# Weighing two groups of key blocks in a row in a two-layer perceiver kernel, with exponentials six double blocks ahead

## The chip, the cores and the metric

The kernel runs on one core of one Trainium2 chip. The metric is the device time of one execution in microseconds (us), as the median of the runs. Engines are called PE (TensorE, matrix products), DVE (VectorE), ACT (ScalarE) and POOL (GpSimd); SP issues DMAs. Each works through its own list in order and meets the others only at semaphores.

## The reference, cut to what matters

Six stages, each added to a residual x of 2 batches of 256 tokens by 256 channels. Stages 0 and 3 are cross attentions over a context of 4096 keys, and the change is inside these two. All is float32.

```
# stage 0, 8 heads of 64 ("plain"); stage 3, 16 heads of 64 ("biased")
q, k, v = xn @ Wq, context @ Wk, context @ Wv
sim     = einsum('bihd,bjhd->bhij', q, k) * scale (+ bias[256, 4096] in stage 3)
out     = softmax(sim) @ v
x       = x + out @ Wo (+ bo in stage 0)
```

Stage 1 is a chunked delta rule, stage 2 a mixture of 15 experts, stage 4 an attention with quantised numbers, stage 5 a recurrent cell over 64 steps.

## The kernel before, in words

`cross_attention` (L161) serves both attention stages. A step m is one pair of heads of one batch: 8 steps in the plain stage and 16 in the biased one. The 4096 keys are 8 groups g of 512; a group is two double blocks kp of 256 keys each, 16 in all. Scores stand with keys on the partitions, so E has 16 slots of 128 x 1024 numbers, one for each double block.

The steps overlap. In the sweep of m (L412 on PE), PE weighs the values with the exponentials of m, computes the scores of m+1, and projects context pieces: the values of m+1 and the keys of m+2. In the text Wg is the weighing of group g (8 products, recorded as 16 instructions), Sg the scores of group g, and Vg and Kg are the projections (pieces) of its values and keys. The order is written out by hand: in each group come W, then in groups 2, 3 and 5 a V piece, then S, then one more piece, by the tables

```
BEFORE_SCORES = {2: ("V", 2), 3: ("V", 3), 5: ("V", 5)}
AFTER_SCORES = {0: ("V", 0), 1: ("V", 1), 2: ("K", 0), 3: ("K", 1), 4: ("V", 4), 5: ("K", 2), 6: ("K", 3), 7: ("K", 4)}
```

After group 7 follows the end of the sweep: V6, the sum over keys (L388), V7, the turning of the peaks (L394), K5, the spreading of the peaks (L399), the output projection (L407), K6, the queries of m+2, and K7.

Three rules decide who waits for whom.

- All pieces go through one PSUM bank (PIECE = 4). A piece waits until ACT has copied the one before it (`piece_kept`, L334).
- Scores alternate between two double banks: Scores of kp wait until those of kp-2 have been copied to E (`scores_kept`, L359). In the biased stage DVE copies them and adds the bias (L559, "out" in the text); in the plain stage ACT copies them (L505).
- After a step's scores, the peak of each query is found by DVE (L573), and each slot of E is lowered by it (DVE, L580), then goes through the exponential (ACT, L510), then is weighed (PE) and summed (POOL, L297). AHEAD = 4 slots are lowered at the end of the sweep. The others are lowered inside the next sweep: at its double block kp DVE lowers slot kp + 4, behind the out of kp; ACT's two exponentials of slots 2g + 4 and 2g + 5 stand in its list behind the copies of the pieces of group g.

The first sweep of a stage only scores, the last only weighs. The last but one has no more keys to compute, so only V pieces. So 6 sweeps of the plain stage and 14 of the biased one are complete.

Of the kernel before, what the change touches and what calls it, by code (L numbers as in the profile page):

```python
# [160 lines left out]
def cross_attention(nc, c, k, tag, wqkv, w_out, b_out, ctx_t, biased, heads, scale):  # L161
# [10 lines left out]
    KG = S2 // NG  # L172
    NP = 2 * NG
    HQ = 4
    AHEAD = 4
    V_PIECES = [piece for piece in PIECES if piece[0] == "V"]
    with ExitStack() as stack:
        def sb(name, shape, dtype=F32):
# [43 lines left out]
        def pieces_of(m):  # L222

            return V_PIECES if isinstance(m, int) and m == END - 2 else PIECES

        def piece_count(m, piece):

            return NP * m + 24 + pieces_of(m).index(piece) + 1
# [7 lines left out]
        def values_count(p, g):  # L236

            return piece_count(p - 1, ("V", g))
# [15 lines left out]
        with nc.Block() as block:  # L254
# [54 lines left out]
            def _(pe):  # L309
# [20 lines left out]
                def piece(m, which):  # L330
                    if which not in pieces_of(m):
                        return
                    kind, g = which
                    pe.wait_ge(piece_kept, piece_count(m, which) - 1)  # L334
                    if kind == "V":
                        values(m + 1, g)
                    else:
                        keys(m + 2, g, PIECE)
# [30 lines left out]
                def weigh(m, g):  # L369
                    pe.wait_ge(piece_kept, values_count(m, g))  # L370
                    if g == 0 and not (isinstance(m, int) and m == START):
                        pe.wait_ge(o_kept, m)
                    for kp in (2 * g, 2 * g + 1):
                        pe.wait_ge(exp_done, NP * m + kp + 1)
                        for h in range(2):
                            for n in range(2):
                                last = pe.matmul(c.ps[n * HD:(n + 1) * HD, OUT, h * S:(h + 1) * S],  # L377
                                                 VS[:, 2 * kp + n, h * HD:(h + 1) * HD], E[:, kp, 2 * h:2 * h + 2, n, :],
                                                 start=(kp == 0 and h == 0), stop=(kp == NP - 1),
                                                 skip_group_check=True)  # L380
                    if g == NG - 1:
                        last.then_inc(weighed, 1)

                def spread_sums(m, scoring):
                    pe.wait_ge(summed, NP * m + NP)
                    if scoring:
                        pe.wait_ge(scores_kept, NP * (m + 1) + NP - 1)
                    pe.matmul(c.ps[:, SUMS_SPREAD, :], c.ones[:, :], FOLD[:, :, :].rearrange("p a n -> p (a n)"),  # L388
                              start=True, stop=True).then_inc(sums_spread, 1)
# [21 lines left out]

                def sweep(m, attending, scoring, more_keys):  # L412
                    for g in range(NG):
                        if attending:
                            weigh(m, g)
                        if scoring:
                            if g in BEFORE_SCORES:
                                piece(m, BEFORE_SCORES[g])
                            scores(m + 1, 2 * g)
                            scores(m + 1, 2 * g + 1)  # L420
                            piece(m, AFTER_SCORES[g])
                    if scoring:
                        piece(m, ("V", 6))
                    if attending:
                        spread_sums(m, scoring)
                    if scoring:
                        piece(m, ("V", 7))
                        turn_peaks(m + 1)
                        piece(m, ("K", 5))
                        spread_peaks(m + 1)  # L430
                    if attending:
                        project(m)
                    if more_keys:
                        piece(m, ("K", 6))
                        queries(m + 2)
                        piece(m, ("K", 7))
# [42 lines left out]
            @block.scalar  # L479
            def _(act):  # L480
                def keys_out(count, g, bank):
                    act.wait_ge(piece_done, count)
                    act.activation(KT[:, g * KG:(g + 1) * KG], c.ps[:, bank, :], ACT.Copy).then_inc(piece_kept, 1)  # L483

                def piece_out(m, which):
                    if which not in pieces_of(m):
                        return
                    kind, g = which
                    count = piece_count(m, which)
                    if kind == "K":  # L490
                        keys_out(count, g, PIECE)
                    else:
                        act.wait_ge(piece_done, count)
                        act.activation(VS[:, 4 * g:4 * g + 4, :].rearrange("p a n -> p (a n)"), c.ps[:, PIECE, :],  # L494
                                       ACT.Copy).then_inc(piece_kept, 1)

                def queries_out(p):
                    act.wait_ge(q_done, p + 1)
                    act.activation(QS[:, :], c.ps[:, QUERIES, 0:S], ACT.Copy, scale=scale).then_inc(q_kept, 1)

                def scores_out(p, kp, attending):
                    act.wait_ge(scores_done, NP * p + kp + 1)
                    if attending:
                        act.wait_ge(summed, NP * (p - 1) + max(kp, 1))
                    act.activation(both(E[:, kp, :, :, :]), scores_bank(kp), ACT.Copy).then_inc(scores_kept, 1)  # L505

                def exponential(p, kp):
                    act.wait_ge(lowered, NP * p + kp + 1)
                    at = both(E[:, kp, :, :, :])
                    act.activation(at, at, ACT.Exp).then_inc(exp_done, 1)  # L510

                def sweep(m, attending, scoring, more_keys):
                    for g in range(NG):
                        if scoring:
                            if g in BEFORE_SCORES:
                                piece_out(m, BEFORE_SCORES[g])
                            if not biased:
                                scores_out(m + 1, 2 * g, attending)
                                scores_out(m + 1, 2 * g + 1, attending)
                            piece_out(m, AFTER_SCORES[g])  # L520
                        if attending and 2 * g + AHEAD < NP:
                            exponential(m, 2 * g + AHEAD)
                            exponential(m, 2 * g + AHEAD + 1)
                    if scoring:
                        piece_out(m, ("V", 6))
                        piece_out(m, ("V", 7))
                        piece_out(m, ("K", 5))
                        exponential(m + 1, 0)
                        piece_out(m, ("K", 6))
                        exponential(m + 1, 1)  # L530
                        if more_keys:
                            queries_out(m + 2)
                        piece_out(m, ("K", 7))
                        exponential(m + 1, 2)
                        exponential(m + 1, 3)

                if b_out is not None:
                    act.dma_start(bo[:, :], b_out.rearrange("(o n) -> o n", o=1)).then_inc(rest_in, 16)
                norm_scalar(c, act, k)

                act.wait_ge(c.ln_std, k + 1)
                keys_out(NP * START + 1, 0, PIECE)
                keys_out(NP * START + 2, 1, PIECE + 1)
                queries_out(START)
                for g in range(2, NG):
                    keys_out(NP * START + g + 1, g, PIECE + g % 4)
                sweep(START - 1, False, True, True)
                with act.Fori(START, END - 2) as m:
                    sweep(m, True, True, True)
                sweep(END - 2, True, True, False)  # L550
                sweep(END - 1, True, False, False)

            @block.vector
            def _(dve):
# [53 lines left out]
                def sweep(m, attending, scoring):  # L608
                    for kp in range(NP):
                        if scoring and kp > 0:  # L610
                            peak(m + 1, kp - 1, 0)
                        if scoring and biased:
                            scores_out(m + 1, kp, attending)
                            if kp > 0:
                                peak(m + 1, kp - 1, 1)
                        if attending and kp + AHEAD < NP:
                            lower(m, kp + AHEAD)
                        if scoring and not biased and kp > 0:
# [11 lines left out]
                    if scoring:  # L630
                        for kp in range(AHEAD):
                            lower(m + 1, kp)
# [1437 lines left out]
```

## Time and profile before

| | |
|---|---|
| median of 3 runs | 2179.23 us (2177.58 to 2181.44) |
| profiled execution | 2181.46 us, of which the span is 2179.7 us |
| PE busy | 1920.6 us (88%) |
| DVE busy | 1632.9 us (75%) |
| POOL busy | 956.5 us (44%) |
| ACT busy | 838.5 us (38%) |
| mean granted TensorE clock | 0.934 of full speed |

A matmul's record is longer than the step to the next one, since matmuls are pipelined. So the cost of a block on PE is read as the distance from its start to the start of the next block; "idle before" counts only the time after the modelled end. Times of the trace count from the start of the span. The plain attention takes about the first 590 us, the biased one runs from about 930 to 2015 us.

### The profile page before, as it was taken

The page shows a single profiled execution, that of the slowest core. Times are in us where ns is not written, and L with a number is a line of the kernel's source. Part 1 is how long each engine was busy: PE and PEld are TensorE (multiplying, and loading weights), DVE is VectorE, ACT ScalarE, POOL GpSimd, SP SyncE. Part 2 cuts the span into 40 slices and gives each one's busy share as a digit, 9 for nine tenths or more (in the row PEclk, how much of TensorE's full clock was granted, in tenths as well). Part 3 has the DMA queues.
Part 4 walks back from the last instruction along what each step waited for, and adds up shares of the span by engine and source line. Part 5 has one row for each costly group of instructions (what it writes and reads, how often), then busy time and mean ns, then how long its engine had stood idle before and what let it go on. Part 6 is the DMA issues. An engine that isn't in the chain of part 4 may idle for free. (4 is left out here: it accounts for less than half of the span.)

```text
span 2179.7 us, 34477 instructions
## 1 busy us (share of the span) xinstructions
PE 1920.6 (88%) x12512; PEld 1311.0 (60%) x12514; DVE 1632.9 (75%) x2131; ACT 838.5 (38%) x1108; POOL 956.5 (44%) x450
## 2 busy tenths in 40 slices
PE   8999999999458889899999999999999999996226
PEld 5666666666238778666666666666666666664124
DVE  3666666668387356689988999889998889987562
ACT  3655665556230135233343333433343333434001
POOL 0454665546550034024655546555465545646200
PEclk9999999999669589999999999999999999998557
DMA  2000100000100062000000000110000000000001
GB/s 104 8 13 12 58 31 12 12 8 6 40 3 1 1 242 77 10 8 8 5 12 12 12 5 7 54 47 12 0 12 12 12 12 0 12 8 5 20 0 49
DMA packets 27717, 52.45 MB, mean 24 GB/s; under 512 B 4227, under 2 KB 15252, under 8 KB 27156
## 3 DMA queue, kind: packets, MB, share of 16 engines
q1 hardware_dynamic: 27200, 51.60, 7.3%
q8 instruction: 34, 0.56, 0.1%
q10 hardware_dynamic: 468, 0.16, 0.0%
q14 instruction: 15, 0.12, 0.0%
HBM read 51.23 MB, written 0.52 MB: 24 GB/s over the span
## 5 line engine op out<-in xcount | busy, mean ns | idle before, releaser
L297 POOL TENSOR_TENSOR biased_sums<-biased_sums,biased_scores 128x1024 f32<-128x1024 f32 x224 | 529.2, 2363 | 210.0 <-ACT biased_scores L510 205.9
L559 DVE TENSOR_TENSOR biased_scores<-ps,bias 128x1024 f32<-128x1024 f32 x256 | 311.0, 1215 | 79.4 <-PE ps L365 79.4
L510 ACT ACTIVATE biased_scores<-biased_scores 128x1024 f32<-128x1024 f32 x256 | 268.2, 1053 | 245.0 <-DVE biased_scores L580 244.0
L573 DVE TENSOR_TENSOR ps<-ps,biased_scores 128x512 f32<-128x512 f32 x480 | 331.6, 691 | 3.6
L580 DVE TENSOR_TENSOR biased_scores<-biased_scores,ps 128x1024 f32<-128x1024 f32 x256 | 304.9, 1210 | 11.9 <-PE ps L399 11.9
L297 POOL TENSOR_TENSOR plain_sums<-plain_sums,plain_scores 128x1024 f32<-128x1024 f32 x112 | 264.6, 2362 | 84.5 <-ACT plain_scores L510 74.7
L325 PEld LDWEIGHTS ps<-weights_again,context_again 128*128 128x128 f32 x2048 | 238.2, 191 | 70.2 <-issue 33.5
L325 PE MATMUL ps<-weights_again,context_again 128*128 128x128 f32 x2048 | 262.4, 281 | 13.1 <-ACT biased_keys L483 11.0
L316 PE MATMUL ps<-context_again,weights_again 128*128 128x512 f32 x512 | 251.3, 613 | 19.5 <-ACT biased_values L494 16.9
L365 PE MATMUL ps<-biased_queries,biased_keys 64*128 64x256 f32 x2048 | 257.3, 390 | 6.6 <-DVE biased_scores L559 5.8
L573 DVE TENSOR_TENSOR ps<-ps,plain_scores 128x512 f32<-128x512 f32 x240 | 167.3, 697 | 115.7 <-ACT plain_scores L505 111.4
L377 PE MATMUL ps<-biased_scores,biased_values 128*64 128x256 f32 x2048 | 250.8, 386 | 1.8 <-ACT biased_scores L510 1.1
L365 PEld LDWEIGHTS ps<-biased_queries,biased_keys 64*128 64x128 f32 x2048 | 186.7, 186 | 63.1 <-DVE biased_scores L559 24.4
L377 PEld LDWEIGHTS ps<-biased_scores,biased_values 128*64 128x64 f32 x2048 | 135.4, 136 | 123.4 <-issue 59.6
L297 POOL TENSOR_TENSOR biased_sums<-biased_scores 128x1024 f32<-128x1024 f32 x16 | 37.8, 2364 | 356.9 <-ACT biased_scores L510 356.9
L483 ACT ACTIVATE biased_keys<-ps 128x512 f32<-128x512 f32 x128 | 76.5, 597 | 280.1 <-PE ps L316 280.1
L316 PEld LDWEIGHTS ps<-context_again,weights_again 128*128 128x128 f32 x512 | 88.0, 189 | 116.7 <-issue 88.3
L580 DVE TENSOR_TENSOR plain_scores<-plain_scores,ps 128x1024 f32<-128x1024 f32 x128 | 152.1, 1211 | 7.0 <-PE ps L399 7.0
L494 ACT ACTIVATE biased_values<-ps 128x512 f32<-128x512 f32 x128 | 75.7, 591 | 178.5 <-PE ps L325 178.5
L505 ACT ACTIVATE plain_scores<-ps 128x1024 f32<-128x1024 f32 x128 | 124.0, 1020 | 43.2 <-PE ps L365 43.2
L325 PEld LDWEIGHTS ps<-weights,context 128*128 128x128 f32 x1024 | 119.1, 191 | 35.7 <-issue 16.4
L325 PE MATMUL ps<-weights,context 128*128 128x128 f32 x1024 | 131.2, 281 | 7.6 <-ACT plain_keys L483 5.5
(356 smaller groups left out, 2304.1 us busy)
## 6 DMA issues: line engine op xcount, KB each, us to landing
context<-in_ctx_t SPq DMA_DIRECT2D x8, 1024.0 KB, 5.4
moe_w<-in_moe_w SPq DMA_DIRECT2D x32, 256.0 KB, 2.8
context_again<-in_ctx_t SPq DMA_DIRECT2D x8, 1024.0 KB, 6.6
weights_again<-in_wqkv SPq DMA_DIRECT2D x45, 128.0 KB, 2.1
bias<-in_fside SPq DMA_DIRECT2D x1, 4096.0 KB, 22.6
biased_w_out<-in_w_out SPq DMA_DIRECT2D x16, 256.0 KB, 2.6
weights<-in_wqkv SPq DMA_DIRECT2D x21, 128.0 KB, 2.1
plain_w_out<-in_w_out SPq DMA_DIRECT2D x8, 256.0 KB, 2.7
```

Of the source, the lines that this page charges most:

```text
L297: pool.tensor_tensor(both(SUM[:, :, :, :]), both((E[:, 0] if kp == 1 else SUM)[:, :, :, :]), both(E[:, kp, :, :, :]), ALU.add).then_inc(su ...
L316: last = pe.matmul(c.ps[:, bank, :], W[:, 1, i, :], CT[:, i, g * KG:(g + 1) * KG], start=(i == 0), stop=(i == DC - 1))
L325: last = pe.matmul(c.ps[:, PIECE, n * P:(n + 1) * P], CT[:, i, g * KG + n * P:g * KG + (n + 1) * P], W[:, 2, i, :], start=(i == 0), stop=( ...
L365: last = pe.matmul(out, KT[half, at:at + P], QS[half, :].rearrange("p (t j) -> p t j", t=2), start=True, stop=True)
L377: last = pe.matmul(c.ps[n * HD:(n + 1) * HD, OUT, h * S:(h + 1) * S], VS[:, 2 * kp + n, h * HD:(h + 1) * HD], E[:, kp, 2 * h:2 * h + 2, n, :],
L483: act.activation(KT[:, g * KG:(g + 1) * KG], c.ps[:, bank, :], ACT.Copy).then_inc(piece_kept, 1)
L494: act.activation(VS[:, 4 * g:4 * g + 4, :].rearrange("p a n -> p (a n)"), c.ps[:, PIECE, :], ACT.Copy).then_inc(piece_kept, 1)
L505: act.activation(both(E[:, kp, :, :, :]), scores_bank(kp), ACT.Copy).then_inc(scores_kept, 1)
L510: act.activation(at, at, ACT.Exp).then_inc(exp_done, 1)
L559: dve.tensor_tensor(E[:, kp, :, :, :].rearrange("p (h t) n j -> p h t (n j)", h=2), scores_bank(kp).rearrange("p (h t n) -> p h t n", h=2, ...
L573: ins = dve.tensor_tensor(to, highest, E[:, kp, :, n, :], ALU.max)
L580: dve.tensor_tensor(at, at, c.ps[:, LOWER, :].rearrange("p (a j) -> p a j", a=HQ).unsqueeze(2) .to_broadcast([P, HQ, 2, P]), ALU.add).then ...
```

## The change

Before even groups PE weighs that group and the next one; before odd groups it weighs none. AHEAD becomes 6: six slots are lowered, and six exponentials are done, at the end of a sweep, and in group g of the next one stand the exponentials of slots 2g + 6 and 2g + 7.

```diff
-    AHEAD = 4
+    AHEAD = 6
@@ PE
                 def sweep(m, attending, scoring, more_keys):
                     for g in range(NG):
-                        if attending:
+                        if attending and g % 2 == 0:
                             weigh(m, g)
+                            weigh(m, g + 1)
                         if scoring:
                             if g in BEFORE_SCORES:
                                 piece(m, BEFORE_SCORES[g])
@@ ACT
                         piece_out(m, ("K", 7))
-                        exponential(m + 1, 2)
-                        exponential(m + 1, 3)
+                        for kp in range(2, AHEAD):
+                            exponential(m + 1, kp)
```

On PE, in the loop of the biased stage, group 3 before: weighing (L377), V3 (L325), scores (L365), K1 (L316).

```order
L316 MATMUL ps<-context_again,weights_again 128x512 x2
L370 REGISTER_ALU
L374 REGISTER_ALU
L377 MATMUL ps<-biased_scores,biased_values 64x256 x4
L374 REGISTER_ALU
L377 MATMUL ps<-biased_scores,biased_values 64x256 x4
L334 REGISTER_ALU
L325 MATMUL ps<-weights_again,context_again 128x128 x8
L350 REGISTER_ALU
L359 REGISTER_ALU
L365 MATMUL ps<-biased_queries,biased_keys 128x2x128 x4
```

The same place now:

```order
L316 MATMUL ps<-context_again,weights_again 128x512 x2
L334 REGISTER_ALU
L325 MATMUL ps<-weights_again,context_again 128x128 x8
L350 REGISTER_ALU
L359 REGISTER_ALU
L365 MATMUL ps<-biased_queries,biased_keys 128x2x128 x4
```

The weighing between the piece K0 (L316, first row) and the piece V3 (L325) has moved to group 2, and the two pieces stand side by side. The same holds for V4 and V5 in groups 4 and 5.

On ACT, in the same loop, from the copy of V5 (L494) on, before: the copies of V5 and K2, two exponentials (L510, slots 14 and 15), the copies of K3 and K4.

```order
L494 ACTIVATE biased_values<-ps 128x512
L482 REGISTER_ALU
L483 ACTIVATE biased_keys<-ps 128x512
L508 REGISTER_ALU
L510 ACTIVATE biased_scores<-biased_scores 128x1024
L508 REGISTER_ALU
L510 ACTIVATE biased_scores<-biased_scores 128x1024
L482 REGISTER_ALU
L483 ACTIVATE biased_keys<-ps 128x512
```

From the copy of V4 (L495) on, now:

```order
L495 ACTIVATE biased_values<-ps 128x512
L509 REGISTER_ALU
L511 ACTIVATE biased_scores<-biased_scores 128x1024
L509 REGISTER_ALU
L511 ACTIVATE biased_scores<-biased_scores 128x1024
L494 REGISTER_ALU
L495 ACTIVATE biased_values<-ps 128x512
L483 REGISTER_ALU
L484 ACTIVATE biased_keys<-ps 128x512
```

The exponentials ahead of the copy of V5 are now those of slots 14 and 15, where they were those of 12 and 13; behind the copy of K2 there are none.

## Rows read from the trace of the kernel before

**Rows 1.** Windows: length, busy us of PE, PEld, DVE, ACT, POOL; PEclk.
```profile
214.52:281.98 67.46, 66.35 (x437) 43.74 (x436) 45.22 (x54) 40.57 (x49) 36.70 (x17) 1.00 0.22 71
1035.09:1103.63 68.54, 66.48 (x438) 43.76 (x437) 62.07 (x69) 25.62 (x33) 36.72 (x17) 1.00 0.03 10
```
**Rows 2.** Waits of PE: total us, times, longest; biased (two rows), then plain stage.
```profile
PE ps L316 <- ACT biased_values L494: 16.7, 42, 0.7
PE ps L325 <- ACT biased_keys L483: 9.6, 14, 0.7
...
PE ps L325 <- ACT plain_keys L483: 4.1, 6, 0.7
```
**Rows 3.** Timeline of PE, biased sweep: start, us, instructions, idle before.
```profile
1035.09 1.95 PE L377 MATMUL ps<-biased_scores,biased_values 128*64 128x256 f32 x16
1036.96 2.00 PE L365 MATMUL ps<-biased_queries,biased_keys 64*128 64x256 f32 x16
1038.89 2.05 PE L325 MATMUL ps<-weights_again,context_again 128*128 128x128 f32 x16
1040.87 1.95 PE L377 MATMUL ps<-biased_scores,biased_values 128*64 128x256 f32 x16
...
1052.72 1.98 PE L316 MATMUL ps<-context_again,weights_again 128*128 128x512 f32 x4 [0.21 <-ACT biased_values L494]
1054.63 1.95 PE L377 MATMUL ps<-biased_scores,biased_values 128*64 128x256 f32 x16
...
1074.71 1.98 PE L316 MATMUL ps<-context_again,weights_again 128*128 128x512 f32 x4 [0.74 <-ACT biased_values L494]
...
1088.82 2.05 PE L325 MATMUL ps<-weights_again,context_again 128*128 128x128 f32 x16 [0.69 <-ACT biased_keys L483]
...
1091.57 2.04 PE L325 MATMUL ps<-weights_again,context_again 128*128 128x128 f32 x16
...
1096.46 1.12 PE L399 MATMUL ps<-biased_peaks_diagonal,ones 128*128 128x512 f32 x2 [0.18 <-DVE biased_peaks_diagonal L594]
```
**Rows 4.** Timeline of PE: the end of W0 in two short windows, and K6.
```profile
1036.21 0.82 PE L377 MATMUL ps<-biased_scores,biased_values 128*64 128x256 f32 x6
...
1036.43 0.60 PE L377 MATMUL ps<-biased_scores,biased_values 128*64 128x256 f32 x4
...
1099.15 1.88 PE L316 MATMUL ps<-context_again,weights_again 128*128 128x512 f32 x4
1100.86 1.03 PE L343 MATMUL ps<-XNT,weights_again 128*128 x4
```
**Rows 5.** Timeline of ACT, same sweep.
```profile
1035.68 1.99 ACT L510 ACTIVATE biased_scores<-biased_scores 128x1024 f32<-128x1024 f32 x2
1040.98 0.60 ACT L494 ACTIVATE biased_values<-ps 128x512 f32<-128x512 f32 x1 [3.30 <-PE ps L325]
...
1073.11 1.06 ACT L510 ACTIVATE biased_scores<-biased_scores 128x1024 f32<-128x1024 f32 x1 [2.40 <-DVE biased_scores L580]
1074.08 0.58 ACT L494 ACTIVATE biased_values<-ps 128x512 f32<-128x512 f32 x1
```
**Rows 6.** Timeline of DVE, same sweep.
```profile
1029.08 4.62 DVE L580 TENSOR_TENSOR biased_scores<-biased_scores,ps 128x1024 f32<-128x1024 f32 x4 [0.62 <-PE ps L399]
...
1038.24 1.22 DVE L559 TENSOR_TENSOR biased_scores<-ps,bias 128x1024 f32<-128x1024 f32 x1 [3.95 <-PE ps L365]
...
1041.11 1.22 DVE L559 TENSOR_TENSOR biased_scores<-ps,bias 128x1024 f32<-128x1024 f32 x1
...
1044.56 1.22 DVE L559 TENSOR_TENSOR biased_scores<-ps,bias 128x1024 f32<-128x1024 f32 x1
...
1082.98 1.21 DVE L559 TENSOR_TENSOR biased_scores<-ps,bias 128x1024 f32<-128x1024 f32 x1
...
1085.49 1.23 DVE L559 TENSOR_TENSOR biased_scores<-ps,bias 128x1024 f32<-128x1024 f32 x1
...
1091.77 3.36 DVE L585 RECIPROCAL biased_shares<-ps 128x512 f32<-128x512 f32 x1 [0.53 <-PE ps L388]
```

## The prediction

> **What bounds the kernel now.** I read the page's busy shares first: PE 88%, DVE 75%. They are means over stages, so next come windows over one complete sweep of each attention [rows 1]. The reader sees that PE is busy for 66.35 of 67.46 us (plain) and 66.48 of 68.54 us (biased), at full granted clock, with DVE at 45 us in the one and 62 us in the other. So PE sets the pace. In the biased stage DVE has only 6.5 us to spare, and it feeds ACT, which feeds PE. Third, what PE waits for: ACT's copies of pieces. The 42 waits of the first row are three in each of 14 biased sweeps, and the 14 of the second are one in each [rows 2]. The timeline shows these places: 0.21 us before K0, 0.74 before K2, 0.69 before V6 [rows 3]. The 0.69 is the pure price of two pieces in a row through one bank: K4 runs, ACT copies for 0.6 us, V6 starts. The 0.74 is another thing. The copy of V5 came at 1074.08, behind the exponential at 1073.11, which had waited for DVE's lowering [rows 5]. So a copy can be late because of its place in ACT's list.
>
> **Prices.** PE, start to next start [rows 3]: W 1.88 and 1.87, S 1.93, V before W 1.98, K before W 1.91. A piece right behind a piece starts 1.98 + 0.69 = 2.67 us after a K, and 2.75 after a V (V6 to V7 is 1091.57 - 1088.82, with a product between them that does not use the bank; by the copy alone, 2.09 + 0.60 + 0.05 = 2.74). ACT starts a V copy 2.09 us after V starts [rows 3, 5] and takes 0.6; a pair of exponentials takes 1.99, one 1.06, and the next instruction follows after 0.97 [rows 5]. DVE: the out of kp starts 1.28 us after its S for an even kp (1038.24 - 1036.96), out 0 to out 1 is 2.87, later ones 3.45 with a lowering between and 2.51 without; a lowering takes 1.2, with steps of 1.13 [rows 6].
>
> **W next to W.** No such pair ran before at full clock. Inside W, each two records are 0.22 us apart (1036.21 to 1036.43), but the last two start at 1036.65 and S only at 1036.96: 0.31 [rows 3, 4]. So 0.10 of W's 1.88 is the passage to another block, and 8 x 0.216 = 1.73 is its own, which leaves 0.05 at its entry. K6, followed by a block of its own tile form, lasts 1.71 (1099.15 to 1100.86), against 1.91 before W [rows 3, 4]. Bounds for two Ws: 3.76 (nothing saved) and 3.44 (both at K6's pace). I take 3.61, from W's own rows: 0.15 saved, four times a sweep, so 0.6 us per sweep. The Trainium skill ("TensorEngine Tiling (Array Packing)", Key Properties) says that changing the tiling mode drains the engine, and the trace agrees with these 0.10 to 0.20 us. By that rule alone the change would only gain.
>
> **The biased sweep now**, from the start of W0 = 0. At the end of the sweep before, six lowerings start at -6.0 (1029.08) and end at 0.9, and ACT does exponentials 2 to 5 from 0.6 to 4.5. W1 needs 2 at 1.8 and 3 at 2.6; they end at 1.65 and 2.6. No stall, but no margin.
> - S0 3.6, V0 5.5, S1 7.5. DVE starts out 0 at 4.9 and out 1 at 7.8, done at 9.0. S1's second half is ready at 8.5 and waits: stall 0.55. Before, W1 stood between S0 and S1 and hid this.
> - V1 10.0, W2 12.0, W3 13.8, V2 15.6, S2 17.6, K0 19.5. The copy of V2 stands behind exponential 9 (lowering 9 ends at 17.6), and is done at 19.2, so the old 0.21 before K0 is gone.
> - V3 directly behind K0: 22.2 instead of 21.4, stall 0.76. S3 24.15.
> - K1 is ready at 26.1. The copy of V3 now stands behind exponential 11. Out 4 could start only at 18.85, since S2 was late; out 5 follows at 22.3, lowering 11 ends at 25.25, exponential 11 at 26.3, the copy at 26.8. K1 starts at 26.9: stall 0.80.
> - W4 28.8, W5 30.6, S4 32.4, V4 34.3, V5 37.1: stall 0.75. S5 39.0. The copy of V5 stands behind exponential 15: out 8 starts at 33.7, out 9 at 37.1, lowering 15 ends at 40.1, the copy at 41.65. K2 is ready at 41.0, starts at 41.7: stall 0.74, as before.
> - W6 43.6, W7 45.4, S6 47.2, K3 49.2, S7 51.1 with 0.2 for out 13, K4 53.2, V6 55.9 (the old 0.75 between them stays).
> - Before, V6 started 53.73 after W0 [rows 1, 3]. Then V6 to L399 was 7.64. DVE has been fed late: out 15 starts at 56.0, its peaks end at 59.2, L399 comes 4.69 behind the reciprocal [rows 3, 6], at 63.9, so 8.0 behind V6. From there to the next W0 7.17 as before.
> The sweep is 71.06 us instead of 68.54: 2.5 more. As a sum: new stalls 0.55 + 0.76 + 0.80 + 0.75 + 0.2 = 3.06, less 0.21 removed and 0.6 saved by W next to W, plus 0.3 at the end. 14 complete sweeps: 35 us.
>
> **The plain sweep now.** ACT copies the scores there, and DVE only has lowerings and peaks, so slots are lowered well ahead: the copies of V3 and V5 (24 and 38 us after W0) find exponentials 11 and 15 done. What is new is V3 behind K0, 0.76, and V5 behind V4, 0.75; the plain V6 behind K4 has the same 0.7 today [rows 2]. Less 0.6: 0.9 a sweep, 5.6 us in 6.
>
> **The other sweeps.** The first ones do not weigh, the last ones only weigh: the order is as before, and the two lowerings more at the end of a sweep are two fewer later. The sweep with V pieces only: in the plain stage 0.75 for V4 and V5 and some 0.3 for two score blocks in a row, less 0.6; in the biased stage DVE sets the pace, as 14 us of its 19 us of lowerings lie in the sweep, now 11, and the later start of S0 takes that back. Together 0.8. POOL sums at 2.4 us a slot, 36.7 of 68.5 us [rows 1]; it ends well before the sweep does. SP's loads wait for the same pieces.
>
> **Sum.** 35 + 5.6 + 0.8 = 41.4 us on the profiled 2181.46 gives 2222.9; on the median of the runs, which is 2.2 lower, 2220.6. I predict 2221 us.
>
> **Rivals.**
> - Only the shared bank counts. The biased copies of V3 and V5 come early enough, and DVE isn't starved: biased 0.76 + 0.75 - 0.21 - 0.6 = 0.7 a sweep, plus plain 5.6: 15 us, 2195. For it: DVE stood idle for 3.95 us before out 0 [rows 6] and now lowers two slots there. Against: S2 and S4 come late on PE, so DVE can't start outs 4 and 8 earlier. Chance 0.12.
> - DVE's chain snowballs: the exponentials of the head slots come late for W1, S1's stall grows to the full 1.3 us from S to out, and the late DVE carries its delay past L399. Then 1.2 us more in each biased sweep, 17 us: 2238. If two Ws also save nothing, 2250. For it: the margins at W1 are 0 to 0.1. Chance 0.12.
> - No change: V3 and V5 cost their 1.5 a sweep, but an earlier V5 copy also removes the 0.74 before K2, and two Ws save 0.32, the lower bound, four times: biased 1.5 - 0.95 - 1.3 = -0.7, plain 0.2, together 9 us less at most, or about zero with the stall of S1. About 2179. Chance 0.05.
> - Faster: the drain is what counts. If ACT's copy between neighbouring pieces lay beside PE's drain, the two new stalls would be under 0.3 each and the rest would be 0.6 + 0.95 gained per biased and 0.6 per plain sweep, less 0.6: 14 x 0.95 = 13 us less, 2166. It decides from the point where a pair of pieces costs less than W next to W saves. Against: the 0.69 before V6 stands in all 14 sweeps [rows 2]. Chance 0.04. The skill's rule on the tiling mode, above, is the one that speaks for it.
> - The granted clock falls since PE idles more. It was 1.00 with 2.1 us idle in a sweep [rows 1]; now it's 4.5 in pieces under 1 us. I give this nothing of its own; it is in the upper end.
>
> **How the numbers follow.** Forecast 0.67, the rivals 0.12, 0.12, 0.05, 0.04. The forecast's own bounds come from two Ws (3.44 to 3.76, so 14 us less to 12 us more over 20 sweeps) and from 0.3 us a sweep on each stall that ends by DVE. The range takes in both near rivals in part: 2193 to 2238. A measurement of this kernel tells 0.2%, about 4 us, from no change. Faster 0.05, same 0.05, slower 0.90.
>
> **What would show it.** Right: 71.1 us between two L399 in the biased stage, 68.4 in the plain; idle of PE near 0.7 before V3, K1, V5, K2 and V6, and 0.5 in S1 behind DVE; none before K0; two Ws in 3.6. Wrong: no idle before K1, or L399 to L399 under 70 us; PE idle over 1 us at W1 or S1; a granted clock under 1.00 in complete sweeps.

## The result and the profile after

The changed kernel takes 2219.1 us (median; 2218.1 to 2220.4) against 2179.2 before: ratio 1.0183, 95% interval 1.0165 to 1.020, so a loss that is clear of the noise. That is 39.9 us more, where 2221 was forecast. The profiled execution took 2220.4 us, with a span of 2218.6.

Windows over one plain and one biased sweep after, with the columns of [rows 1]:

```profile
216.00:284.44 68.44, 65.95 (x438) 43.97 (x436) 45.44 (x54) 40.35 (x49) 36.75 (x17) 1.00 0.22 70
1116.54:1187.61 71.07, 66.64 (x438) 43.81 (x436) 62.24 (x70) 25.41 (x34) 36.79 (x17) 1.00 0.03 9
```

The lengths are 68.44 and 71.07 us, against 67.46 and 68.54. Busy times hardly differ: PE does the same work in a longer sweep. The granted clock is 1.00 in both.

The waits of PE in the biased stage after (total us, times, longest), to be read against [rows 2]:

```profile
PE ps L316 <- ACT biased_values L495: 23.2, 43, 0.7
PE ps L325 <- ACT biased_keys L484: 19.2, 28, 0.7
PE ps L325 <- ACT biased_values L495: 10.3, 15, 0.7
PE ps L365 <- DVE biased_scores L560: 10.3, 19, 1.4
PE ps L399 <- DVE biased_peaks_diagonal L595: 8.6, 15, 3.9
```

The keys row went from 14 waits to 28: V3 behind K0 is the new one. The third row is new: V5 behind V4. The fourth now has one wait of 0.37 us in each complete sweep, S1's; its other five lie in the sweep with V pieces only. The timeline of PE from W0 to L399 of one biased sweep (start, us, instructions, idle before) shows each step:

```profile
1115.67 3.73 PE L377 MATMUL ps<-biased_scores,biased_values 128*64 128x256 f32 x32
1119.33 2.00 PE L365 MATMUL ps<-biased_queries,biased_keys 64*128 64x256 f32 x16
...
1123.24 1.14 PE L365 MATMUL ps<-biased_queries,biased_keys 64*128 64x256 f32 x8
1124.74 1.14 PE L365 MATMUL ps<-biased_queries,biased_keys 64*128 64x256 f32 x8 [0.37 <-DVE biased_scores L560]
1125.81 2.05 PE L325 MATMUL ps<-weights_again,context_again 128*128 128x128 f32 x16
1127.79 3.67 PE L377 MATMUL ps<-biased_scores,biased_values 128*64 128x256 f32 x32
1131.39 2.05 PE L325 MATMUL ps<-weights_again,context_again 128*128 128x128 f32 x16
...
1135.30 1.98 PE L316 MATMUL ps<-context_again,weights_again 128*128 128x512 f32 x4
1137.97 2.05 PE L325 MATMUL ps<-weights_again,context_again 128*128 128x128 f32 x16 [0.69 <-ACT biased_keys L484]
...
1142.68 1.98 PE L316 MATMUL ps<-context_again,weights_again 128*128 128x512 f32 x4 [0.73 <-ACT biased_values L495]
...
1152.86 2.05 PE L325 MATMUL ps<-weights_again,context_again 128*128 128x128 f32 x16 [0.69 <-ACT biased_values L495]
...
1157.50 1.98 PE L316 MATMUL ps<-context_again,weights_again 128*128 128x512 f32 x4 [0.66 <-ACT biased_values L495]
...
1166.86 2.30 PE L365 MATMUL ps<-biased_queries,biased_keys 64*128 64x256 f32 x16
1169.09 1.98 PE L316 MATMUL ps<-context_again,weights_again 128*128 128x512 f32 x4
1171.76 2.05 PE L325 MATMUL ps<-weights_again,context_again 128*128 128x128 f32 x16 [0.69 <-ACT biased_keys L484]
...
1179.56 1.13 PE L399 MATMUL ps<-biased_peaks_diagonal,ones 128*128 128x512 f32 x2 [0.33 <-DVE biased_peaks_diagonal L595]
```

To be read in it, in this order: two Ws in 3.66 (the first pair) or 3.60 to 3.61 us (the others), where two took 3.75 or 3.76; S1's second half waiting for DVE, so that S1 takes 2.57 us (1123.24 to 1125.81) where an S takes 1.93; no idle before K0 at 1135.30, where 0.21 stood; the new 0.69 before V3, 0.73 before K1 and 0.69 before V5; 0.66 before K2 and 0.69 before V6, which were there before (0.74 and 0.69) [rows 3]; S7 in 2.23 us instead of 1.93 (1166.86 to 1169.09); and L399 0.33 late, where it was 0.18. V6 comes 56.1 us after W0.

The wait before K1 is in ACT's list. Its timeline there:

```profile
1137.82 1.05 ACT L511 ACTIVATE biased_scores<-biased_scores 128x1024 f32<-128x1024 f32 x1
1141.09 1.06 ACT L511 ACTIVATE biased_scores<-biased_scores 128x1024 f32<-128x1024 f32 x1 [2.22 <-DVE biased_scores L581]
1142.05 0.58 ACT L495 ACTIVATE biased_values<-ps 128x512 f32<-128x512 f32 x1
```

V3 was computed by 1140.02 (1137.97 + 2.05), but exponential 11 waited 2.22 us for DVE's lowering, and V3's copy stood behind it until 1142.05.

### The profile page after: what moved, and what is told of

Same layout as the page of the kernel before. It is cut to its first block and busy times, and to the rows that moved or that the text cites. A ratio compares the mean times of both kernels' runs of the same rounds, so it can differ in the third digit from the quotient of the medians.

```text
span 2218.6 us, 34465 instructions
## 1 busy us (share of the span) xinstructions
PE 1916.5 (86%) x12512; PEld 1311.8 (59%) x12514; DVE 1636.8 (74%) x2131; ACT 833.6 (38%) x1108; POOL 957.5 (43%) x450
## 5 line engine op out<-in xcount | busy, mean ns | idle before, releaser
L325 PEld LDWEIGHTS ps<-weights_again,context_again 128*128 128x128 f32 x2048 | 238.2, 192 | 93.4 <-ACT biased_keys L484 45.4
L325 PE MATMUL ps<-weights_again,context_again 128*128 128x128 f32 x2048 | 262.5, 281 | 33.0 <-ACT biased_keys L484 20.6
L365 PE MATMUL ps<-biased_queries,biased_keys 64*128 64x256 f32 x2048 | 265.8, 393 | 12.7 <-DVE biased_scores L560 11.2
L316 PE MATMUL ps<-context_again,weights_again 128*128 128x512 f32 x512 | 251.4, 614 | 25.8 <-ACT biased_values L495 23.2
L377 PE MATMUL ps<-biased_scores,biased_values 128*64 128x256 f32 x2048 | 238.2, 384 | 1.5 <-ACT biased_scores L511 0.7
L365 PEld LDWEIGHTS ps<-biased_queries,biased_keys 64*128 64x128 f32 x2048 | 184.3, 186 | 81.3 <-issue 32.0
L377 PEld LDWEIGHTS ps<-biased_scores,biased_values 128*64 128x64 f32 x2048 | 138.7, 137 | 108.7 <-issue 38.4
L316 PEld LDWEIGHTS ps<-context_again,weights_again 128*128 128x128 f32 x512 | 88.1, 189 | 123.0 <-issue 79.8
L495 ACT ACTIVATE biased_values<-ps 128x512 f32<-128x512 f32 x128 | 75.6, 591 | 193.5 <-PE ps L325 193.5
L325 PEld LDWEIGHTS ps<-weights,context 128*128 128x128 f32 x1024 | 119.1, 192 | 45.9 <-ACT plain_keys L484 21.2
L325 PE MATMUL ps<-weights,context 128*128 128x128 f32 x1024 | 131.3, 281 | 16.5 <-ACT plain_keys L484 9.6
```

The costliest lines, as they stand in the source:

```text
L316: last = pe.matmul(c.ps[:, bank, :], W[:, 1, i, :], CT[:, i, g * KG:(g + 1) * KG], start=(i == 0), stop=(i == DC - 1))
L325: last = pe.matmul(c.ps[:, PIECE, n * P:(n + 1) * P], CT[:, i, g * KG + n * P:g * KG + (n + 1) * P], W[:, 2, i, :], start=(i == 0), stop=( ...
L365: last = pe.matmul(out, KT[half, at:at + P], QS[half, :].rearrange("p (t j) -> p t j", t=2), start=True, stop=True)
```

## Experiments

The length of a sweep is read below from the rows of L399 (its number moves by a few lines with the code), which runs once a sweep, recorded as two instructions 0.56 us apart: first and last start, less 0.56, over the number of sweeps between.

**AHEAD back at 4, weighing still in pairs.**

```diff
-    AHEAD = 6
+    AHEAD = 4
```

> The changed kernel with AHEAD back at 4: two groups weighed in a row, but only four slots exponentiated ahead. Theory A (AHEAD = 6 is what pays for the pairs: the second W of a pair needs exponentials that DVE lowers two double blocks later): W3 waits about 4 us for exponential 7, W5 and W7 about 1.8 us each, and a biased sweep is near 78 us instead of 71.07; the plain sweep, where DVE lowers well ahead, stays within 0.3 us of 68.44. Total about 2320 us. Theory B (the loss of the change comes from the six lowerings at the end of the sweep, which fill DVE there): the biased sweep comes back to under 70 us, total about 2200 us.

Measured 2396.9 us in a single run, before 2181.0 on the same chip. The plain sweep is 68.9 us, the biased one 81.9. The row of L399 (one biased sweep between four records) and the timeline of PE from W2 to K0, with the second half of W5:

```profile
L399 PE MATMUL ps<-biased_peaks_diagonal,ones x4: 592/645/697, 1299.8 to 1382.3; 128*128 128x512 f32 x4
```

```profile
1319.12 1.95 PE L377 MATMUL ps<-biased_scores,biased_values 128*64 128x256 f32 x16
1322.35 1.08 PE L377 MATMUL ps<-biased_scores,biased_values 128*64 128x256 f32 x8 [1.28 <-ACT biased_scores L511]
1325.81 1.98 PE L377 MATMUL ps<-biased_scores,biased_values 128*64 128x256 f32 x8 [2.37 <-ACT biased_scores L511]
1327.71 3.79 PE L325 MATMUL ps<-weights_again,context_again 128*128 128x128 f32 x16
1331.43 2.27 PE L365 MATMUL ps<-biased_queries,biased_keys 64*128 64x256 f32 x16
1333.63 1.98 PE L316 MATMUL ps<-context_again,weights_again 128*128 128x512 f32 x4
...
1347.44 1.08 PE L377 MATMUL ps<-biased_scores,biased_values 128*64 128x256 f32 x8 [1.71 <-ACT biased_scores L511]
```

Theory A: W3 waits for exponentials 6 and 7 (1.28 and 2.37 us), and W5 and W7 wait 1.71 us each. Six slots ahead are what makes pairs bearable in the biased stage. The plain sweep came out 0.47 us above 68.44, a little more than the 0.3 allowed. The size was missed, since something was added that nobody had written down: behind the 2.37 us of idle the same eight records take 1.98 us, not 1.08, and V2 3.79, not 2.05. The windows of this stretch have the granted clock (third column from the end):

```profile
1300.00:1320.00 20.00, 19.63 (x126) 13.09 (x128) 13.65 (x16) 8.69 (x12) 10.53 (x5) 1.00 0.11 33
1325.30:1325.80 0.50, 0.00 (x0) 0.00 (x0) 0.00 (x0) 0.45 (x1) 0.00 (x0) 0.50 0.00 0
1325.80:1330.00 4.20, 4.19 (x18) 3.06 (x19) 0.00 (x0) 0.00 (x0) 2.35 (x1) 0.50 0.00 0
1332.10:1332.50 0.40, 0.40 (x8) 0.35 (x6) 0.00 (x0) 0.03 (x1) 0.00 (x0) 1.00 0.00 0
```

It fell from 2.4 to 1.2 GHz while PE still waited, and was back by 1332.1, nearly 7 us later. Over that time PE lost 2.9 us: 0.9 in the eight records, 1.7 in V2 (1327.71 to 1331.43 is 3.72 for 1.98) and 0.3 in S2 (2.20 for 1.93). The rest of the 10.9 us above 71.07 is the waits: counted from start to start W2 and W3 lost 4.1 us, W4 with W5 and W6 with W7 1.9 each. So the waits were near what was expected, and the clock is what was left out.

**AHEAD = 6 alone, one group weighed at a time.**

```diff
# kernel before
-    AHEAD = 4
+    AHEAD = 6
-                        exponential(m + 1, 2)
-                        exponential(m + 1, 3)
+                        for kp in range(2, AHEAD):
+                            exponential(m + 1, kp)
```

> The kernel before with AHEAD = 6 alone, weighing one group at a time as before. Theory A (the lowering two slots earlier moves nothing that PE waits for: ACT's exponentials of a group still wait for DVE's work of the same double block): biased sweep 68.5 us, plain sweep 67.5 us, total 2179 us within 5; the 0.74 us before K2 stays. Theory B (six lowerings at the end are part of the loss): biased sweep 69 us or more, total over 2187 us.

Measured 2175.7 us against 2181.0, ratio 0.9978 (0.9967 to 0.9989). L399 over two sweeps, this kernel and the kernel before:

```profile
L399 PE MATMUL ps<-biased_peaks_diagonal,ones x6: 592/644/697, 1095.4 to 1233.0; 128*128 128x512 f32 x6
```

```profile
L399 PE MATMUL ps<-biased_peaks_diagonal,ones x6: 592/644/697, 1096.5 to 1234.1; 128*128 128x512 f32 x6
```

Both are (137.6 - 0.56) / 2 = 68.5 us, and the plain sweep is 67.47 in both. So AHEAD = 6 by itself moves no complete sweep: theory A. The last but one biased sweep, which has V pieces only and where DVE sets the pace, is 2.0 us shorter (64.8 against 66.8), which fits the two slots that DVE now lowers in its idle time before it starts. The two profiled spans differ by 6.8 us. Of these, 2.0 are this sweep, and 3.7 lie behind the last L399 of the biased stage (189.2 against 192.9 us), where nobody changed anything and where the eight executions of this document differ by as much among themselves (last section). So beyond the 2.0 us it is open how much of the gain comes from AHEAD = 6.

**Copies between the exponentials, weighing in pairs.** In the biased stage ACT copies V2, V3 and V5 between the two exponentials of the group before.

```diff
-                            if g in BEFORE_SCORES:
+                            if g in BEFORE_SCORES and not (biased and attending):
                                 piece_out(m, BEFORE_SCORES[g])
...
                             exponential(m, 2 * g + AHEAD)
+                            if scoring and biased and g + 1 in BEFORE_SCORES:
+                                piece_out(m, BEFORE_SCORES[g + 1])
                             exponential(m, 2 * g + AHEAD + 1)
```

> The changed kernel; in the biased stage ACT copies V2, V3 and V5 between the two exponentials of the group before, instead of behind both. Theory A (the waits before K1 and K2 are the copies' place in ACT's list, behind exponentials 11 and 15): both waits vanish (0.73 + 0.66 us), the 0.69 us before V3 and V5 stay, the biased sweep falls from 71.07 to about 69.5 us, 14 x 1.5 = 21 us less: about 2198 us. Theory B (DVE sets the pace of the biased sweep now, and PE's waits only show it): the time taken away before K1 and K2 comes back before S3, S5 or L399, and the sweep stays over 70.7 us, total over 2213 us.

Measured 2200.8 us, ratio 1.0094 (1.0079 to 1.011). L399 over two sweeps, then PE from S3 to K1 and from V5 to K2:

```profile
L399 PE MATMUL ps<-biased_peaks_diagonal,ones x6: 592/644/697, 1105.0 to 1244.6; 128*128 128x512 f32 x6
```

```profile
1136.47 2.00 PE L365 MATMUL ps<-biased_queries,biased_keys 64*128 64x256 f32 x16
1138.40 1.98 PE L316 MATMUL ps<-context_again,weights_again 128*128 128x512 f32 x4
...
1148.58 2.05 PE L325 MATMUL ps<-weights_again,context_again 128*128 128x128 f32 x16 [0.69 <-ACT biased_values L495]
1150.56 2.00 PE L365 MATMUL ps<-biased_queries,biased_keys 64*128 64x256 f32 x16
1152.49 1.98 PE L316 MATMUL ps<-context_again,weights_again 128*128 128x512 f32 x4
```

A sweep is 69.5 us. K1 follows S3 without idle, and K2 too (1150.56 to 1152.49), while the 0.69 before V3 and V5 stays. So 1.5 us a sweep are gained without touching PE's order. Not all of that is loss of the change: the wait before K2 was there before it. Theory B falls: DVE, at 62 us of 69.5, didn't ask for the time elsewhere, and the waits that it ends, 0.37 us in S1 and 0.33 before L399, are as they were.

**The same edit of ACT's list in the kernel before.** (AHEAD = 4, one group at a time.)

> The kernel before (single weighings, AHEAD = 4) with the same edit of ACT's list: V2, V3 and V5 copied between two exponentials in the biased stage. Theory A: the 0.21 us before K0 and the 0.74 us before K2 go, the biased sweep falls from 68.54 to 67.7 us, the end of the sweep gives back 0.1 to 0.2; 14 x 0.8 = 11 us less: about 2168 us. Theory B (DVE, busy for 62 of 68.5 us, is at its limit): the waits move to DVE's products (S or L399) and the sweep stays within 0.2 us of 68.54, total 2177 to 2181 us.

Measured 2164.8 us against 2181.0, ratio 0.9928 (0.9914 to 0.9941).

```profile
L399 PE MATMUL ps<-biased_peaks_diagonal,ones x6: 592/644/697, 1095.5 to 1231.2; 128*128 128x512 f32 x6
```

```profile
1139.30 2.00 PE L365 MATMUL ps<-biased_queries,biased_keys 64*128 64x256 f32 x16
1141.23 1.98 PE L316 MATMUL ps<-context_again,weights_again 128*128 128x512 f32 x4
```

A sweep is 67.6 us instead of 68.5. K2 now starts 1.93 us behind S5, where it was 2.73: the 0.74 us before K2 was the place of V5's copy behind an exponential. The 0.21 before K0 is gone too, and L399 waits 0.30 instead of 0.18.

With the copies between the exponentials in both kernels, pairs cost 69.5 - 67.6 = 1.9 us a sweep, against 2.5 with the copies behind. So the place of the copies accounts for 0.6 us of the loss that the change brings, and PE's order, by the shared bank and by DVE, for the other 1.9.

**Pairs with the pieces spread.** The changed kernel (AHEAD = 6, copies in their old place), with no two pieces side by side in groups 0 to 7 (the list of all pieces, put in the same order, is left out here):

```diff
+BEFORE_SCORES = {2: ("V", 2), 4: ("V", 4), 6: ("K", 2)}
+AFTER_SCORES = {0: ("V", 0), 1: ("V", 1), 2: ("V", 3), 3: ("K", 0), 4: ("V", 5), 5: ("K", 1), 6: ("K", 3), 7: ("K", 4)}
```

> The changed kernel (pairs, AHEAD = 6) with the same 11 pieces in the sweep put where no two are neighbours: W0 W1 S0 V0 S1 V1 W2 W3 V2 S2 V3 S3 K0 W4 W5 V4 S4 V5 S5 K1 W6 W7 K2 S6 K3 S7 K4. Theory A (the bank shared by neighbouring pieces is what the plain stage loses, and W next to W saves 0.6 us there): no wait before V3 and V5, plain sweep 66.9 us, so below the 67.46 of single weighing; biased sweep about 70.2, since scores two blocks apart make PE wait about 1 us for DVE before the second halves of S1, S3 and S5. Total about 2197 us. Theory B (W next to W saves nothing in a whole sweep, and the plain loss is of another cause): plain sweep 67.5 us or more.

Measured 2204.5 us, ratio 1.0111 (1.0094 to 1.0128). L399 over one plain and two biased sweeps, and the waits for DVE in the biased stage:

```profile
L399 PE MATMUL ps<-plain_peaks_diagonal,ones x4: 592/644/697, 138.9 to 206.4; 128*128 128x512 f32 x4
...
L399 PE MATMUL ps<-biased_peaks_diagonal,ones x6: 592/645/697, 1095.7 to 1237.2; 128*128 128x512 f32 x6
```

```profile
PE ps L365 <- DVE biased_scores L560: 33.5, 44, 1.0
PE ps L325 <- ACT biased_keys L484: 9.6, 14, 0.7
```

The plain sweep is 66.9 us, 1.5 below the changed kernel's 68.44 and 0.55 below the 67.46 of single weighing. This is both halves of the plain sum at once: two pairs of neighbouring pieces cost 1.5 us, and four pairs of Ws save 0.55. The biased sweep is only 0.6 us shorter, 70.5: PE now waits for DVE before the second halves of S1, S3 and S5 (0.37, 0.96, 0.96 us), because scores stand closer together than DVE's 6.9 us for a group. So in the biased stage pairs lost in both orders of pieces that were run; other orders were not. The total is 7.5 us above the expected 2197: 4 of them are the 0.3 us by which each biased sweep is longer than expected, and the rest was in the expectation, whose own sweeps add up to about 2200.

**What the runs point to.** The plain stage with pairs and spread pieces; the biased stage with single weighings and the copies between the exponentials; AHEAD = 6 in both.

> What the runs point to: plain stage with pairs and spread pieces, biased stage with single weighings and the copies of V2, V3 and V5 between two exponentials, AHEAD = 6 in both. Theory A (the parts are independent): plain sweep 66.9 us, biased sweep 67.6 us, the sweep with V pieces only 2 us shorter as with AHEAD = 6 alone; about 2160 us, 1% below the kernel before. Theory B (AHEAD = 6 takes from DVE at the end of the sweep what the new place of the copies gave): biased sweep 68 us or more, total over 2166 us.

Measured 2161.3 us (2157.1 to 2165.6) against 2180.1, ratio 0.9907 (0.9891 to 0.9924): faster than both kernels.

```profile
L406 PE MATMUL ps<-biased_peaks_diagonal,ones x6: 592/644/697, 1098.0 to 1233.4; 128*128 128x512 f32 x6
```

The biased sweep is 67.4 us, the plain one 66.92: theory A, the parts are independent. Against the copies' edit alone (0.9928) the two intervals overlap, so the total does not prove the last 3 us; the sweeps do. In its profiled execution, the slowest of the four, the stages between the two attentions took 431.5 us, against 425.1 in the kernel before, though no one touched them; the granted clock (third column from the end) was lower there:

```profile
532.90:964.40 431.50, 336.54 (x2283) 270.11 (x2282) 260.39 (x440) 112.67 (x198) 111.04 (x75) 0.80 0.15 48
```

```profile
535.60:960.70 425.10, 329.38 (x2282) 263.08 (x2281) 260.21 (x440) 112.61 (x198) 111.04 (x75) 0.83 0.14 49
```

## Why the prediction was right

The direction, the places and the size were right. The biased sweep as a sum, in us against the kernel before. Measured is from start to start of the blocks, the measure that the prediction names for costs; the idle column reads up to 0.3 us less, as it counts from a modelled end.

| term | forecast | measured |
|---|---|---|
| S1's second half waits for DVE | +0.55 | +0.64 |
| V3 behind K0 | +0.76 | +0.76 |
| K1, V3's copy behind exponential 11 | +0.80 | +0.80 |
| V5 behind V4 | +0.75 | +0.75 |
| S7 waits for out 13 | +0.2 | +0.30 |
| K0, its old wait gone | -0.21 | -0.27 |
| K2, V5's copy behind exponential 15 | 0 | -0.08 |
| W next to W, four pairs | -0.6 | -0.54 |
| end of the sweep | +0.3 | +0.16 |
| sum | +2.55 | +2.52 |

- **What bounds.** PE in both stages, with ACT's copies ending its waits: confirmed: the busy time of a sweep is unchanged and the waits grew.
- **Two Ws.** 3.61 forecast; 3.60 to 3.61 for three pairs and 3.66 for the first. The spread pieces show the saving in a whole sweep, 0.55 of 0.6 us.
- **S1.** The second half starts 1.50 us after the first, where without a wait it starts after 0.97 (1042.75 to 1043.72 before), so it comes 0.53 us late. The forecast of 0.55 met that. But the eight records behind the wait then take 1.07 us instead of 0.96, which makes 0.64; the prediction left those 0.1 us out, here and in S7.

```profile
1042.75 2.00 PE L365 MATMUL ps<-biased_queries,biased_keys 64*128 64x256 f32 x16
1043.72 1.03 PE L365 MATMUL ps<-biased_queries,biased_keys 64*128 64x256 f32 x8
```

- **Copies behind exponentials 11 and 15.** Both waits are there, and both are gone when only ACT's list is edited. The prediction set K2 down as unchanged at 0.74, a number of the idle column; from start to start it was 0.80 before and is 0.72.
- **The end of the sweep.** L399 came 7.8 behind V6, not 8.0, and V6 at 56.1, not 55.9. That the sum met 2.52 within 0.03 is partly luck: single terms missed by up to 0.14, and these misses cancel.
- **The plain sweep.** 0.9 forecast, 0.98 seen.
- **The sweeps with V pieces only.** 0.8 forecast for the two together, 1.5 seen. The plain one was put at 0.45 and lost 1.2; half of that is the wait for L399 at its end, which grew from 2.66 to 3.24 us and which the prediction did not count.
- **Sum.** The trace gives 14 x 2.53 + 6 x 0.98 = 41.3 us in the complete sweeps and 1.5 in the other two, so the attention stages lost about 43 us, a little more than forecast. The span grew by only 38.9 us, since behind the biased stage the profiled execution was 3.7 us shorter, as the last section tells. So the forecast 41.4 lies near the 39.9 of the medians partly by luck.

Of the rivals, "only the shared bank counts" was wrong in its own terms. It gave 0.7 us a biased sweep with the wait before K2 still there. The kernel with copies between the exponentials has 69.5 - 68.5 = 1.0 without that wait, where the rival would then give about 0. What it leaves out is DVE: S1, S7 and the end of the sweep, together 1.1 us. "DVE's chain snowballs" did not come, but the margin was used up: in the sweep above, exponential 3 ended at about 1118.27, W1's second half, which needs it, started at 1118.32, and the first pair took 0.06 us more than the others.

## What to carry to other kernels

When an order is changed, look for what the moved block stood between: here W's 1.9 us hid a 0.7 us hand-over of a shared PSUM bank between two pieces. Look also at where a copy that frees a bank stands in its engine's list: behind an instruction that waits for a third engine it comes late. Three such copies moved ahead gave 0.7%, more than any regrouping here; by PE's rows V5's copy gave 0.8 of the 0.95 us a sweep. And a walk through one period, row by row on three engines, forecast the length of a sweep within 0.1 us, and most of its terms too.

## What the runs showed of the hardware

- A block on TensorE behind a block of other tile form cost 0.1 to 0.2 us more than behind one of its own: two Ws in a row took 3.60 us instead of 3.76, and four such pairs saved 0.55 us in a plain sweep. No run separates the form of the tiles from other differences between the blocks. It agrees in kind with the rule that the prediction cites from the Trainium skill ("TensorEngine Tiling (Array Packing)", Key Properties), that a change of the tiling mode drains the engine; the size is from these rows.
- With AHEAD = 4 and pairs, TensorE waited 1.28 us, worked for 1.1 and waited 2.37; before the second wait was over the granted clock was 0.50, and stayed so for nearly 7 us. Waits of 1.71 us, once in each later pair, left it at 1.00, and so did the 0.7 us pauses of the changed kernel, five in a sweep.
- Stages that nobody touched differ between executions. From the last L388 of the biased stage to the end of the span, before and after:

```profile
2030.05:2179.70 149.65, 68.89 (x234) 45.03 (x236) 77.99 (x216) 13.89 (x24) 0.29 (x1) 0.63 0.07 25
```

```profile
2072.70:2218.60 145.90, 65.73 (x234) 42.59 (x236) 78.03 (x216) 13.89 (x24) 0.29 (x1) 0.63 0.08 26
```

The instructions are the same, and only the busy times of PE (3.2 us) and its weight loads differ. In the last stage some stretches ran at the lower clock before: from 2160 to 2170 the granted clock was 0.78, and 1.00 in the matching stretch after. From the last L399 of the biased stage to the end, the eight executions of this document took 192.9 (before), 189.2 (after), and in the order of the experiments 189.5, 189.2, 192.3, 190.0, 193.1 and 189.7 us. What sets this was not tried. A difference of 0.2% between two profiled executions is thus read from the stage that was changed, never from the span.
